# Second feed-forward of a macaron block: batches 0 to 3 through a list of rows sorted by expert

## Chip, cores and metric

One core of one Trainium2 chip. The time is the device time of one execution in microseconds. A run of the kernel before took 1052.49 us (median of three, 1050.71 to 1056.52).

## What is computed

A block of three residual parts over x of shape (8, 512, 128), 8 batches of 512 tokens: half a feed-forward, attention, half a feed-forward again.

```python
x = x + 0.5 * ffn(layernorm(x), ...)
x = x + attn(layernorm(x), ...)
x = x + 0.5 * ffn(layernorm(x), ...)

def ffn(x, gate_w, gate_b, w1, b1, w2, b2, w3, b3):   # 8 experts, 128 x 128 each
    logits = einsum('bsd,de->bse', x, gate_w) + gate_b
    probs = softmax(logits, axis=1)                   # over the tokens of a batch
    vals, idx = top_k(probs, 2)
    h = relu(x @ w1[e] + b1[e]); h = relu(h @ w2[e] + b2[e])
    y = relu(h @ w3[e] + b3[e])                       # for every expert e
    w_tok, ind = the chosen probabilities and the choice, per token and expert
    v = einsum('ebso,bse->eo', y, w_tok)              # one vector per expert
    return einsum('bse,eo->bso', ind, v)
```

The output of an expert for a token counts only through the sum v, weighted with the token's probability for that expert. It is zero for all but the two experts a token chose. The attention has 16 heads of 64 on one key and value head.

## The kernel before

Five engines run programs written by hand; each works in its own order and waits on semaphores. Bias and relu follow each product, and products are made exact enough by splitting both sides into a high and a low part: a layer is three products per 512 tokens (high weights with high data, low weights with high data, high weights with low data).

**Feed-forward.** Its unit is one expert on two batches (a pair), 1024 tokens. Each of the two feed-forwards has 32 units (4 pairs x 8 experts), all dense: every expert sees every token. A unit is 18 products of 128 x 512. TensorE (PE) makes layer 1, VectorE (DVE) makes high and low part of its result (`split1`, L1479 and L1485), PE layer 2, ScalarE (ACT) takes it and rounds it (`relu2`, L1162 and L1166), GpSimd (POOL) makes the low part (`split2`, L686), PE layer 3, and DVE multiplies with the token weights and sums (`reduce3`, L1576). The token weights of a unit are broadcast by a DMA from memory (`load_wb`, L511), into one of eight buffers.

The order of the units is written out by `unit_steps` (L410), which every engine walks: in step u stand layer 1 of unit u+2 with its split, layer 2 of unit u+1, layer 3 of unit u, and then whatever `TAIL` (L382) puts behind step u: the last of the attention (reciprocals, scale, out-projection), the turning of the normalized batches, and the choice of experts for batches 4 to 7. That for batches 0 to 3 is made in the attention.

**PSUM** is a ring of four pairs of banks; the uses are numbered in PE's order, and a use waits until the one four before it is drained.

**Attention.** It runs in 32 quads of four heads (g = 0 to 31, NQ = 32, four per batch). In each, PE makes for eight units the scores of quad g+1 for the row maxima (taken by DVE, L1728) and the scores of quad g (exponentials by ACT, L1356), then the sums of quad g-1 (L1011) and the weighing of the values (L1038). Even quads have projections of q besides, and one in four has k, v and the out-projection (L1050). POOL adds the exponentials (`add_exp`, L627), six sums per quad, which PE's sums need. Exponential u of quad g waits for a sum of quad g-1, because it overwrites what that sum reads.

**SP** issues nearly all DMAs, in one order: in each quad the sums of the last one are spread (`spread_sums`, four transfers, L570), and their reciprocals, taken by DVE, are sent and broadcast (`send_reciprocals`, L576 and L580). After the last quad `late_weights` (L539) mixes the same for quad 31 with the loads of the token weights.

## Time and profile before

| | us |
|---|---|
| median of three runs | 1052.49 |
| lowest, highest | 1050.71, 1056.52 |
| profiled execution, its span (first to last instruction) | 1048.3 |
| TensorE busy | 1015.9 (97%) |
| VectorE, GpSimd, ScalarE busy | 763.9, 700.0, 632.1 |

No time of the profiled execution beyond its span is on the page; what lies around it is taken as the median less the span, 4.2 us. The span falls into the first feed-forward (to some 175 us), the attention (to 877 us, 32 quads of about 16 to 29 us) and the second feed-forward. PE's sum of busy time counts overlapping instructions once; two products in a row start 0.23 us apart although each is listed with 0.39. "SPq" rows are the issuing of DMAs by SP, not their transfer.

### The profile page before, as it was taken

Reading aid. Unit: us, or ns where it says so; the run is one execution under the profiler, and the core shown is the slowest. Engines: PE = TensorE matmul, PEld = TensorE weight load, DVE = VectorE, ACT = ScalarE, POOL = GpSimd, SP = SyncE. Lnnn points to the kernel's source line nnn. Section 1 sums busy time; section 2 is a strip of 40 time slices with the busy share of each in tenths; the row PEclk is TensorE's granted clock in tenths of the full one; section 3 lists DMA queues with packets and bytes.
Section 4 is the critical chain, followed back from the end, with each engine's and each line's share of the span. In section 5 each row is a group of like instructions: output and inputs, shape, how many; then the busy total and the mean of one; then the engine's idle time right before and its main releaser. Section 6 shows DMA issues by size and latency. Waiting matters only on the chain.

```text
span 1048.3 us, 18768 instructions
## 1 busy us (share of the span) xinstructions
PE 1015.9 (97%) x7176; PEld 661.9 (63%) x7176; DVE 763.9 (73%) x1027; ACT 632.1 (60%) x900; POOL 700.0 (67%) x369
## 2 busy tenths in 40 slices
PE   7999998899999999999999999999999999998996
PEld 6676886545657566556655665745565565776884
DVE  6879998877875676567576587546757636779996
ACT  4785556756754565456475477467746456775553
POOL 5555655766886588488488578756849757565653
PEclk9999999999999999999999999999999999999999
DMA  5721520000100100001001010001000103521612
GB/s 169 237 86 58 183 84 21 1 2 23 42 23 22 42 24 22 22 23 43 22 23 43 3 42 23 22 25 40 22 23 23 42 25 102 182 81 49 209 67 81
DMA packets 30253, 59.62 MB, mean 57 GB/s; under 512 B 10437, under 2 KB 15702, under 8 KB 30166
## 3 DMA queue, kind: packets, MB, share of 16 engines
q1 hardware_dynamic: 30096, 58.41, 18.4%
q8 instruction: 58, 0.95, 0.4%
q14 instruction: 29, 0.24, 0.1%
q10 hardware_dynamic: 70, 0.02, 0.0%
HBM read 55.27 MB, written 2.62 MB: 55 GB/s over the span
## 4 chain that ended last, share of the span: by engine, by line
PE 83%; DVE 10%; ACT 2%; issue 2%; POOL 2%; DMA 0%; DVEq 0%; ACTq 0%; POOLq 0%
PE ring L1038 20%; PE ring L972 6%; PE ring L1050 6%; PE ring L996 5%; PE ring L1002 5%; PE ring L998 5%; PE ring L1000 5%; PE ring L742 4%; PE ring L748 4%; PE ring L744 4%; PE ring L1011 3%; PE ring L766 2%; PE ring L765 2%; PE ring L768 2%; DVE ring L1576 2%
## 5 line engine op out<-in xcount | busy, mean ns | idle before, releaser
L1728 DVE TENSOR_REDUCE mx<-ring 128x2 f32<-128x1024 f32 x248 | 290.3, 1226 | 64.1 <-PE ring L972 64.1
L627 POOL TENSOR_TENSOR sum_picksT<-sum_picksT,P_wb 128x1024 f32<-128x1024 f32 x128 | 310.7, 2427 | 18.9 <-POOL sum_picksT L627 0.9
L1356 ACT ACTIVATE P_wb<-ring 128x1024 f32<-128x1024 f32 x256 | 262.1, 1026 | 54.2 <-PE ring L1002 24.6
L627 POOL TENSOR_TENSOR sum_picksT<-P_wb 128x1024 f32<-128x1024 f32 x64 | 167.0, 2610 | 167.8 <-ACT P_wb L1356 167.8
L686 POOL TENSOR_TENSOR R<-t,R 128x512 fp32r<-128x512 f32 x124 | 162.1, 1308 | 124.5 <-ACT R L1166 121.2
L1038 PE MATMUL ring<-P_wb,t 128*32 128x512 f32 x2048 | 228.4, 593 | 0.0
L1038 PEld LDWEIGHTS ring<-P_wb,t 128*32 128x32 f32 x2048 | 74.0, 110 | 138.6 <-issue 120.0
L1368 ACT COPY OZ<-ring 128x512 f32<-128x512 f32 x64 | 37.4, 585 | 157.3 <-PE ring L1038 148.6
L1166 ACT CAST R<-t 128x512 fp32r<-128x512 f32 x124 | 76.9, 620 | 74.6 <-PE ring L748 68.2
L972 PE MATMUL ring<-R 64*128 64x512 f32 x512 | 104.8, 407 | 1.0 <-ACT P_wb L1344 0.7
L996 PE MATMUL ring<-R 64*128 64x512 f32 x512 | 102.0, 393 | 1.5 <-DVE MR L1733 1.5
L1000 PE MATMUL ring<-R 64*128 64x512 f32 x512 | 101.1, 390 | 0.0
L998 PE MATMUL ring<-R 64*128 64x512 f32 x512 | 101.0, 390 | 0.0
L1002 PE MATMUL ring<-MR,NEG 64*128 64x512 f32 x496 | 98.3, 392 | 0.0
L1162 ACT ACTIVATE t<-ring,bcol 128x512 f32<-128x512 f32 x124 | 84.8, 684 | 20.8 <-PE ring L768 20.3
L1576 DVE SCALAR_TENSOR_TENSOR ring<-ring,nb,P_wb 128x1024 f32<-128x1024 f32 x62 | 80.0, 1290 | 13.3 <-PE ring L748 13.2
L742 PE MATMUL ring<-R,whi 128*128 128x512 f32 x252 | 81.5, 404 | 6.1 <-DVE MR L1485 1.8
L748 PE MATMUL ring<-R,whi 128*128 128x512 f32 x252 | 79.6, 396 | 0.0
L744 PE MATMUL ring<-R,wlo 128*128 128x512 f32 x252 | 79.6, 396 | 0.0
L972 PEld LDWEIGHTS ring<-R 64*128 64x128 f32 x512 | 48.2, 184 | 36.9 <-issue 24.9
L1753 DVE TENSOR_TENSOR OT_xnT<-OZ,rzb 128x1024 f32<-128x1024 f32 x32 | 70.0, 2188 | 0.0
L996 PEld LDWEIGHTS ring<-R 64*128 64x128 f32 x512 | 47.9, 184 | 34.6 <-ACT P_wb L1356 29.7
(199 smaller groups left out, 1529.9 us busy)
## 6 DMA issues: line engine op xcount, KB each, us to landing
P_wb<-wd SPq DMA_DIRECT2D x64, 512.0 KB, 4.8
rzb<-rzd SPq DMA_DIRECT2D x64, 256.0 KB, 3.9
xs<-in_L_attn_x SPq DMA_DIRECT2D x8, 256.0 KB, 5.2
zrc<-SZ SPq DMA_DIRECT2D x128, 2.0 KB, 1.7
out<-xs SPq DMA_DIRECT2D x8, 256.0 KB, 2.7
sum_picksT<-in_L_ffn_w SPq DMA_DIRECT2D x2, 512.0 KB, 5.6
MR<-mT SPq DMA_DIRECT2D x62, 4.0 KB
t<-in_L_ffn_w SPq DMA_DIRECT2D x1, 512.0 KB, 7.3
```

The lines of the kernel that those rows point to most:

```text
L627: pool.tensor_tensor(US[:, g % 2, c, :, :], first, PU[:, TPB * c + t, :, :], ALU.add).then_inc(s_ua, 1)
L686: pool.tensor_tensor(low[:, k, :], t2[:, k, :], high[:, k, :].bitcast(F32), ALU.subtract).then_inc(s["h2_ready"], 1)
L742: pe.matmul(pair[:, k, :], whi[:, layer, e, :], high[:, k, :], start=True, stop=False)
L744: pe.matmul(pair[:, k, :], wlo[:, layer, e, :], high[:, k, :], start=False, stop=False)
L972: mm = pe.matmul(banks[:, par, :], QH[g % len(QH)][rows, c, P * j:P * (j + 1)], KH[rows, g // QUADS % 2, :], start=True, stop=True)
L996: pe.matmul(banks[:, par, :], KH[rows, kv, keys], QH[g % len(QH)][rows, c, :], start=True, stop=False)
L998: pe.matmul(banks[:, par, :], KH[rows, kv, keys], QL[g % len(QL)][rows, c, :], start=False, stop=False)
L1000: pe.matmul(banks[:, par, :], KL[rows, kv, keys], QH[g % len(QH)][rows, c, :], start=False, stop=False)
L1002: mm = pe.matmul(banks[:, par, :], less[rows, :], MR[rows, g % 2, c, :], start=False, stop=True)
L1038: mm = pe.matmul(weigh_bank(g, c)[row:row + SLOT, :], Vn[:, g // QUADS % 2, t, d:d + SLOT], PU[:, TPB * c + t, par, :], start=(t == 0), st ...
L1356: act.activation(PU[:, u, :, :], ring[slot(("scores", g, u))][:, :, :], ACT.Exp, scale=SCALE).then_inc(s_exp, 1)
L1728: dve.tensor_reduce(mx[:, :, u] if g else mx0_unit[:, u // TPB, :, 0, u % TPB, 0], ring[slot(("max", g, u))][:, :, :], AX.X, ALU.max).then ...
```

## The change

Batches 0 to 3 of the second feed-forward no longer go through all experts. The two rows each token has (one per chosen expert) are put into a list in memory, sorted by expert, each expert's share padded to full tiles of 512 rows. With 4096 rows and 8 experts that is at most 15 tiles (`RT`), a number fixed when the kernel is built. Two tiles form a unit: 8 sorted units (`RU`), the last with one tile, then the 16 dense ones of batches 4 to 7. The parts:

- In the first feed-forward the list is filled with zeros by five DMAs from SP (`zero_rows`).
- In quad 24 (`CHOICE0`; 28 before) DVE chooses the experts and counts per row what was chosen before it; two small products (`ranks`) give the sums over partitions; in quad 25 `place_rows` works out each row's place in the list, in quad 29 `tile_tables` the expert and the biases of each tile. Turning, logits and probabilities of batches 0 to 3 move two quads ahead.
- ACT writes the normalized rows with their eight token weights beside them into a ring of six (`fill_rows`, quads 25 to 29), and POOL sends them by indirect DMAs of 128 rows of 136 values (`send_rows`): one group of three tiles (six DMAs) behind the sums of quad 25, two groups behind those of 26 and of 28, and the last, of one tile, behind those of 30. POOL then copies the weights of unit 0.
- In the second feed-forward a sorted unit needs: its rows loaded (`load_sorted`, SP), turned (`gather`, eight transposes on PE), split (`sorted_high` on ACT, `sorted_low` on DVE), its token weights picked out by DVE, written and broadcast (`spread_row_weights`, SP), and the weights of its two tiles' experts copied by POOL to a fixed place (`copy_weights`), since they are known only at run time. The token-weight buffers are a ring of three there. Split and reduction go in halves, because the two tiles have different biases.
- `TAIL` has the rest of the attention and the choice for batches 4 to 7 behind steps 0 to 7.

The core of the diff:

```diff
+    TS = 4 * P
+    RT = 2 * TPB * TPB * P // TS + E - 1
+    RU = (RT + 1) // 2
+    UNITS_OF = (NU, RU + NU // 2)
...
+        PLACES0, TILES0 = NQ - 7, NQ - 3
+        ROWS_FILLED = {NQ - 7: (0, 1), NQ - 6: (2,), NQ - 5: (3,), NQ - 4: (4,), NQ - 3: (5,)}
+        ROWS_SENT = {NQ - 7: (0,), NQ - 6: (1, 2), NQ - 4: (3, 4), NQ - 2: (5,)}
...
+        TAIL = {0: [("copy", 3), ("scale", NQ - 1), ("normal", 4)],
+                1: [("copy", 4), ("out", B - 1), ("turn", 4), ("normal", 5)],
...
+                7: [("choose", 1), ("choose", 2), ("choose", 3), ("picks", 1)]}
...
-                steps = [("layer1", 0), ("split", 0), ("sums", NQ - 1), ("normal", 2), ("layer1", 1), ("split", 1), ("layer2", 0)]
+                steps = [("copy", 1), ("layer1", 0), ("split", 0), ("sums", NQ - 1), ("gather", 1), ("layer1", 1), ("split", 1),
+                         ("reciprocals", NQ - 1), ("gather", 2), ("layer2", 0), ("copy", 2)]
...
+                if routed(f, u + 3):
+                    steps.append(("gather", u + 3))
...
+            def spread_row_weights(u):
+                n = len(halves_of(1, u))
+                sp.wait_ge(s_rw, u + 1)
+                sp.dma_start(wg[u, 0:n].rearrange("k p j -> p k j"), row_weights[u % 2][:, 0:n, :]).then_inc(s_rwd, 16)
+                sp.wait_ge(s_rwd, 16 * (u + 1))
...
             def late_weights():
+                s = F[1]
                 spread_sums(NQ - 1)
+                load_sorted(1)
+                spread_row_weights(0)
                 send_reciprocals(NQ - 1)
+                for u in range(2, RU):
+                    load_sorted(u)
+                    spread_row_weights(u - 1)
+                spread_row_weights(RU - 1)
+                send_weights(1, 1, GW[1][1]["wT"])
...
+            def send_rows(n):
+                pool.wait_ge(s_fill, n + 1)
...
+                for i, t in enumerate(FILLS[n]):
+                    for k in range(2):
+                        place = TPB * TPB * k + t
+                        pool.indirect_dma_start(out=xg[:, :], out_offset=bass.IndirectOffsetOnAxis(ap=row_of[:, place:place + 1], axis=0),
+                                                in_=ring_rows[:, FILL * (n % 2) + i, :], in_offset=None).then_inc(s_sent[n % 2], 16)
+            def copy_weights(u):
...
+                for k in halves_of(1, u):
+                    e = pool.value_load(expert_int[0:1, 2 * u + k:2 * u + k + 1], min_val=0, max_val=E - 1)
+                    ins = pool.tensor_copy(tile_weights(u, k).rearrange("p l h o -> p (l h o)"),
+                                           wex[:, bass.ds(e, 1), :, :, :].rearrange("p e l h o -> p (e l h o)"))
+                ins.then_inc(s_tw, 1)
...
             def layer1(f, u):
+                if routed(f, u):
+                    pe.wait_ge(s_rxl, u + 1)
+                    pe.wait_ge(s_tw, u + 1)
...
+            def gather(u, pair):
+                pe.wait_ge(s_sorted[u % 2], 16 * (u // 2 + 1))
+                for half in halves_of(1, u):
+                    mm = turn(pair[:, half, :], lambda j: sorted_of(u)[:, half, j, 0:P])
+                mm.then_inc(s_rx, 1)
```

TensorE at the start of the second feed-forward; `P_wb,t` is the weighing of quad 31, `sum_picksT,ones` are its sums, `ident` rows are transposes, and a layer is three or six rows. Before:

```order
L1038 MATMUL ring<-P_wb,t 32x512 x32
L742 MATMUL ring<-R,whi 128x512 x2
L744 MATMUL ring<-R,wlo 128x512 x2
L748 MATMUL ring<-R,whi 128x512 x2
L1011 MATMUL ring<-sum_picksT,ones 32x512 x4
L742 MATMUL ring<-R,whi 128x512 x2
L744 MATMUL ring<-R,wlo 128x512 x2
L748 MATMUL ring<-R,whi 128x512 x2
L765 MATMUL ring<-R,whi 128x512
L766 MATMUL ring<-R,wlo 128x512
L768 MATMUL ring<-R,whi 128x512
```

And now:

```order
L1234 MATMUL ring<-sum_picksT,ones 32x512 x4
L1075 MATMUL ring<-ident,sum_picksT 128x128 x8
L959 MATMUL ring<-R,tile_weights 128x512 x2
L961 MATMUL ring<-R,tile_weights 128x512 x2
L965 MATMUL ring<-R,tile_weights 128x512 x2
L1075 MATMUL ring<-ident,sum_picksT 128x128 x8
L986 MATMUL ring<-R,first_tile_weights 128x512
L987 MATMUL ring<-R,first_tile_weights 128x512
L989 MATMUL ring<-R,first_tile_weights 128x512
```

Between the sums and layer 2 of unit 0 (L765 before, L986 now) there was one layer; now there are two gathers and a layer between them.

SP after the last quad's reciprocals; `rows_by_expert` is the sorted list, `weights_by_row` the picked token weights. Before:

```order
L570 DMA zrc<-SZ 16x1x32 x4
L511 DMA P_wb<-wd 128x1024 x2
L576 DMA rzd<-zrc 64x32
L580 DMA rzb<-rzd 64x1024 x2
L511 DMA P_wb<-wd 128x1024 x12
```

And now:

```order
L737 DMA zrc<-SZ 16x1x32 [waits reciprocals,sums_taken]
L737 DMA zrc<-SZ 16x1x32 x3
L679 DMA sum_picksT<-rows_by_expert 128x2x544 [waits sums_filled]
L685 DMA weights_by_row<-tile_tables 128x2x4 [waits row_weights_ready]
L692 DMA P_wb<-weights_by_row 128x1024 [waits exp_added,pv_done,row_weights_written]
L743 DMA rzd<-zrc 64x32 [waits reciprocals]
L747 DMA rzb<-rzd 64x1024 [waits quad_scaled,reciprocals_written]
L747 DMA rzb<-rzd 64x1024
L679 DMA sum_picksT<-rows_by_expert 128x2x544 [waits row_weights_ready,sorted_turned,sums_filled]
```

The load for gather 1 stands behind the spreading of quad 31's sums, that for gather 2 behind its reciprocals.

POOL from the sums of quad 31 on; `tile_weights` are the copied weights, `h_low` and R the low parts ahead of layer 3. Before:

```order
L627 TENSOR_TENSOR sum_picksT<-P_wb 128x1024
L627 TENSOR_TENSOR sum_picksT<-sum_picksT,P_wb 128x1024 x2
L686 TENSOR_TENSOR R<-t,R 128x512 x4
L660 TENSOR_TENSOR R<-sum_picksT,R 128x512
L686 TENSOR_TENSOR R<-t,R 128x512 x2
```

And now:

```order
L794 TENSOR_TENSOR sum_picksT<-P_wb 128x1024
L794 TENSOR_TENSOR sum_picksT<-sum_picksT,P_wb 128x1024 x2
L889 TENSOR_LOAD tile_tables
L889 ISA x2
L890 ISA
L890 COPY tile_weights<-wex 128x768
L889 TENSOR_LOAD tile_tables
L889 ISA x2
L890 ISA
L890 COPY tile_weights<-wex 128x768
L856 TENSOR_TENSOR h_low<-t,R 128x512 x2
L889 TENSOR_LOAD tile_tables
```

A copy for two tiles now stands between the low parts of one unit and those of the next.

## Rows read from the trace of the kernel before

**Rows 1.** Page of the profile, busy time of each engine and share of the span

```profile
PE 1015.9 (97%) x7176; PEld 661.9 (63%) x7176; DVE 763.9 (73%) x1027; ACT 632.1 (60%) x900; POOL 700.0 (67%) x369
```

**Rows 2.** Windows: second feed-forward to unit 15; columns PE, PEld, DVE, ACT, POOL busy, clock, DMA

```profile
877.00:973.00 96.00, 91.36 (x427) 69.57 (x427) 78.58 (x101) 64.17 (x117) 53.86 (x40) 1.00 0.38 123
```

**Rows 3.** Timeline (start, duration us, engine, line): one dense unit, 975.4 to 979.6

```profile
975.41 0.63 PE L742 MATMUL ring<-R,whi 128*128 128x512 f32 x2
...
975.68 1.29 DVE L1576 SCALAR_TENSOR_TENSOR ring<-ring,nb,P_wb 128x1024 f32<-128x1024 f32 x1 [0.24 <-PE ring L748]
...
976.30 2.59 POOL L686 TENSOR_TENSOR R<-t,R 128x512 fp32r<-128x512 f32 x2 [1.59 <-ACT R L1166]
...
979.61 0.63 PE L742 MATMUL ring<-R,whi 128*128 128x512 f32 x2
```

**Rows 4.** Timeline, DVE: the end of the last unit

```profile
1037.17 0.20 DVE L1688 TENSOR_REDUCE vv<-vacc 128x8 f32<-128x40 f32 x1
```

**Rows 5.** Timeline, PE: out-projection of quad 30, eight transposes, sums of quad 31

```profile
844.89 7.41 PE L1050 MATMUL ring<-wos,OT_xnT 128*128 128x128 f32 x64
...
867.84 1.09 PE L854 MATMUL ring<-ident,xn 128*128 128x128 f32 x8
...
879.44 1.06 PE L1011 MATMUL ring<-sum_picksT,ones 128*32 128x512 f32 x8 [1.04 <-POOL sum_picksT L627]
```

**Rows 6.** Timeline, ACT and the DMA issues of SP behind those sums

```profile
880.56 0.59 ACT L1362 COPY SZ<-ring 128x512 f32<-128x512 f32 x1 [3.11 <-PE ring L1011]
...
881.17 2.44 SPq L570 DMA_DIRECT2D zrc<-SZ  x4
```

**Rows 7.** DMA issues, 860 to 1048: count, KB each, median us from issue to landing

```profile
P_wb<-wd SPq DMA_DIRECT2D x32, 512.0 KB, 5.0
...
rzd<-zrc SPq DMA_DIRECT2D x2, 8.0 KB, 1.7
```

**Rows 8.** Timeline, DVE: split of two 128x1024 as four 128x512, and a scale

```profile
807.62 2.84 DVE L1722 SCALAR_TENSOR_TENSOR R<-ring,bcol,R 128x512 fp32r<-128x512 f32 x4 [1.34 <-ACT R L1337]
...
888.99 1.79 DVE L1753 TENSOR_TENSOR OT_xnT<-OZ,rzb 128x1024 f32<-128x1024 f32 x1
```

**Rows 9.** Timeline, POOL: operations with one input or none

```profile
0.27 0.11 POOL L1878 MEMSET const-float32-1.0<- 128x1 f32 x1
...
1.19 0.29 POOL L614 TENSOR_SCALAR_AFFINE_SELECT ident<-ident 128x128 f32<-128x128 f32 x1 [0.24 <-POOL ident L612]
```

**Rows 10.** Windows, 25 to 35; columns as in rows 2

```profile
25.00:30.00 5.00, 3.64 (x10) 2.49 (x10) 4.93 (x7) 2.24 (x5) 0.77 (x2) 0.74 0.42 156
30.00:35.00 5.00, 5.00 (x21) 4.01 (x21) 4.96 (x14) 2.05 (x4) 2.04 (x3) 0.91 1.01 288
```

**Rows 11.** Timeline, POOL: first sum of quads 26 to 31, with the idle time before it

```profile
753.17 2.40 POOL L627 TENSOR_TENSOR sum_picksT<-P_wb 128x1024 f32<-128x1024 f32 x1 [2.23 <-ACT P_wb L1356]
...
782.54 2.40 POOL L627 TENSOR_TENSOR sum_picksT<-P_wb 128x1024 f32<-128x1024 f32 x1 [14.53 <-ACT P_wb L1356]
...
800.09 2.40 POOL L627 TENSOR_TENSOR sum_picksT<-P_wb 128x1024 f32<-128x1024 f32 x1 [1.42 <-ACT P_wb L1356]
...
821.01 2.40 POOL L627 TENSOR_TENSOR sum_picksT<-P_wb 128x1024 f32<-128x1024 f32 x1 [3.81 <-ACT P_wb L1356]
...
839.12 2.40 POOL L627 TENSOR_TENSOR sum_picksT<-P_wb 128x1024 f32<-128x1024 f32 x1 [2.28 <-ACT P_wb L1356]
...
863.47 2.40 POOL L627 TENSOR_TENSOR sum_picksT<-P_wb 128x1024 f32<-128x1024 f32 x1 [9.58 <-ACT P_wb L1356]
```

**Rows 12.** Timeline, ACT: the exponentials of quad 30

```profile
836.86 9.17 ACT L1356 ACTIVATE P_wb<-ring 128x1024 f32<-128x1024 f32 x8 [0.75 <-POOL sum_picksT L627]
```

**Rows 13.** Timeline, DVE: choice of experts in quad 28, first and last, next row maxima

```profile
810.58 0.27 DVE L1616 TENSOR_REDUCE tm<-ring 128x16 f32<-128x128 f32 x1
...
814.50 0.37 DVE L1610 TENSOR_TENSOR wtk<-ind,ring 128x128 f32<-128x128 f32 x1
...
817.83 9.34 DVE L1728 TENSOR_REDUCE mx<-ring 128x2 f32<-128x1024 f32 x8 [1.51 <-PE ring L972]
```

More of the change, by code:

```diff
@@ new lines, in macaron_kernel @@
+        before = tables[:, 0:P]
+        ring_rows = tables[:, P:P + 2 * FILL * ROW].rearrange("p (t c) -> p t c", c=ROW)
+        up_to = [tables[:, P + 192 * k:P + 192 * (k + 1)] for k in range(2)]
+        products = tables[:, 4 * P:6 * P].rearrange("p (k t e) -> p k t e", k=2, e=E)
+        row_of_all = tables[:, 6 * P:7 * P].rearrange("p (t e) -> p t e", e=E)
+        LEFT = P + 2 * FILL * ROW
+        count_up = tables[:, LEFT:LEFT + 2 * E]
+        running = [tables[:, LEFT + 2 * E + 12 * k:LEFT + 2 * E + 12 * (k + 1)] for k in range(4)]
@@ new lines, in macaron_kernel @@
+        first_choice, second_choice = (lg0[:, P * k:P * (k + 1)].rearrange("p (t e) -> p t e", e=E) for k in range(2))
+        chosen_by_p, counts, before_p, tiles_full, first_row = (lg0[:, 2 * P + E * k:2 * P + E * (k + 1)] for k in range(5))
+        counts_and_before = lg0[:, 2 * P + E:2 * P + 3 * E]
+        full = lg0[:, 2 * P + 5 * E:2 * P + 9 * E].rearrange("p (e k) -> p e k", k=4)
+        row_sums = lg0[:, 2 * P + 9 * E:2 * P + 13 * E].rearrange("p (k t) -> p k t", k=2)
+        row_of = lg0[:, S - 4 * E:S].bitcast(I32)
@@ L692, in units @@
                         split2(f, arg)
+                    elif stage == "copy":
+                        copy_weights(arg)
                     elif stage == "turn":
@@ L871, in early_gate @@
                     else:
-                        turn_weights(1, 0, bank[:, 0:P])
+                        pe.wait_ge(s_places, 1)
+                        pe.wait_ge(s_const, 5)
+                        pe.matmul(bank[:, 0:E], ones[:, :], chosen_by_p, start=True, stop=True)
+                        pe.matmul(bank[:, E:2 * E], before, chosen_by_p, start=True, stop=True).then_inc(s["picks_transposed"], 1)
             def first_turns():
-                s = F[1]
                 wait_drained(pe, "first_turns")
-                for b in range(2):
-                    pe.wait_ge(s["xn_done"], b + 1)
-                    turn(ring[slot("first_turns")][:, b, :], lambda k: xn[:, b, k, :]).then_inc(s["xn_transposed"], 1)
+                gather(0, ring[slot("first_turns")])
             def units(f):
@@ L894, in units @@
                             sums(arg, bank)
+                        elif stage == "gather":
+                            gather(arg, unit_pair(f, stage, arg))
                         elif stage == "turn":
@@ L1115, in attention @@
                         elif step == "first_turns":
[L1116 removed]
+                            pass
                         elif step == "out":
@@ L1405, in attention @@
                     early_gate(g, 0)
-                    if g == NQ - 1:
-                        for b2 in range(2):
-                            act.wait_ge(F[1]["xn_transposed"], b2 + 1)
-                            act.copy(xh[:, b2, :], ring[slot("first_turns")][:, b2, :]).then_inc(F[1]["x_high"], 1)
                     if g:
```

655 lines of the change are left out of this document (444 added, 211 removed).

## The prediction, made blind

> **What bounds the kernel now.** I read the page first: TensorE is busy 97% of the span [rows 1]. Then the windows: over the half of the second feed-forward that the change rewrites, TensorE is busy 91.4 of 96.0 us and VectorE 78.6, at full clock [rows 2]. The timeline of one dense unit shows the pace: its 18 products take from 975.41 to 979.61, 4.2 us, 1.4 a layer. VectorE needs three passes of 1.29 (the reduction is one), so it has almost nothing to spare [rows 3]. Beside it stands the order of the changed kernel, which I went through wait by wait: on a path that crosses engines what counts is who stands behind whom. The last unit ends at 1037.17 [rows 4].
>
> **What goes.** 16 dense units become 8 sorted ones, of which one is half: 8.5 units x 4.2 = 35.7 us of products. This is the whole gain. I count it from S, the start of the sums of quad 31 (879.44 before [rows 5]), to the end of the reduction of the seventeenth dense unit before (975.68 + 1.29 [rows 3] + the accumulator's 0.1 = 977.1, so S + 97.6) and of unit 8, the first dense one, after. From there both have 15 dense units and the same end (977.1 to 1037.17).
>
> **Head of the second feed-forward.** TensorE's order is now: layer 1 of unit 0, sums, gather 1, layer 1 of unit 1, gather 2, and only then layer 2 of unit 0. From S: ScalarE has the sums at 881.15, SP issues four small transfers until 883.61 [rows 6], S + 4.2. Only behind them comes the load of sorted rows 1; it has 0.56 MB, and I give it the 5.0 of the 0.5 MB transfers [rows 7]: 9.2. Gather (eight transposes) 1.1 [rows 5], ScalarE's high part over 1024 columns 1.1 (the exponentials' pace, 9.17 for 8 [rows 12]), VectorE's low part 1.3 [rows 3]: 12.7. Layer 1 1.4, its split, now four passes, 2.8 [rows 8]: 16.9. Now VectorE scales quad 30, 1.8 [rows 8], and inverts the sums of quad 31 (small, left out): 18.7. SP stands waiting for that inverse: write 1.7 [rows 7], two issues of 0.6 [rows 6], and behind them the load of sorted rows 2, 5.0: 26.6. Gather 1.1: layer 2 of unit 0 starts at S + 27.7. All of it is one path; nothing runs beside it but the split of unit 0 and a weight copy.
>
> **The steps.** POOL's order is: low parts of unit u+1, copy of the weights of unit u+3, and layer 1 of unit u+3 waits for that copy, with layer 2 of unit u+2 behind it. The high part of unit u+1 is written only after layer 3 of unit u. In the dense unit POOL's two low parts end at 976.30 + 2.59 = 978.9, 3.5 after layer 3 was issued (975.41) [rows 3]; the 1.59 that POOL idles ahead of them is that wait. So each step is a ring: 3.5, copies K, three layers 4.2. For K no row has the operation: two copies of 768 columns and two values read from a table. A POOL pass with one input takes 0.29 for 128 columns, an almost empty one 0.11 [rows 9]: 0.11 + 768 x 0.18/127 = 1.2 each. The read lies between nothing and 1.7 (a small transfer [rows 7]); I take 0.35, near nothing, since it moves four bytes. K = 3.1, bounds 2.0 (copies at 1.0, reads free) and 7.1 (copies as two-input passes of 1.84, between 1.3 a 512 pass [rows 3] and 2.40 a 1024 one [rows 11], reads at 1.7).
> TensorE then idles some 5 us in each ring. In the first feed-forward, where it is busy 3.64 of 5 us, the clock falls: 0.74 and then 0.91 of full over ten us [rows 10]. At half clock 0.26 x 5 x 2 + 0.09 x 5 x 2 = 3.5 us, in which half is lost: 1.7. I charge 1.7 per ring; bounds 0 and 4.2 (all three layers at half clock, 1.2 GHz).
> The Trainium skill (TensorE: Matmul & The Clock Gate, "Why this matters for your kernels") warns of exactly this: idle gaps between bursts of products send the array back to half rate. The rows of the first feed-forward bear it out; by the opposite reading, clock never lost, the sum is 10 us lower.
> The first ring from 27.7: ScalarE still has the high part of gather 2 (1.1), four passes of 0.6 [rows 6], 2.5; POOL's second low part 1.3; K 3.1; 4.2 + 1.7: layer 3 of unit 0 is issued at 41.6. Ring = 3.5 + 3.1 + 4.2 + 1.7 = 12.5: 54.1. The second ring holds the out-projection, 7.3 [rows 5], a turn 0.4, a gather 1.1 and the three layers, 4.2, 13.1 in all at full clock: 67.2. Two more: 92.2. In the fifth K is halved (unit 7 has one tile): 10.9, 103.1. Unit 6 needs no copy: 4.2, 107.3. VectorE alone would need, per sorted unit, 1.3 + 0.6 for the sorted rows, 2.8 for the split and 1.7 for two reductions, 6.4: it is covered, as are ScalarE and the gathers.
>
> **From the sorted to the dense units.** The choice for batches 4 to 7 is now squeezed into steps 5 to 7. Reduction of unit 6 1.7, inverse and probabilities 0.9, their turn 0.4, first links 1.2, split of unit 9 2.6, half reduction 0.9: 115.0. Ten links of 0.33 (14 passes from 810.58 to 814.87 [rows 13]), turn and copy 0.6, 118.9; write of the weights 1.7 (as the small write of rows 7), broadcast 5.0, reduction 1.4: 127.0. Before, this chain ran beside units that had their weights; now the first dense reduction waits for it. 127.0 - 97.6 = +29.4.
>
> **In the attention.** VectorE gets 22 memsets (0.1 each, my value from POOL's 0.11 [rows 9]) and six links of 0.33 in quad 24, 4.2 us, beside the choice moved there. In quad 28 it idled 1.51 behind the same choice [rows 13]: +2.7, bounds 0 and 4.2; in this phase row maxima run at TensorE's pace and regain nothing.
> POOL sends 32 times 128 rows: 6 behind quad 25, 12 behind 26, 12 behind 28, 2 behind 30, then copies K. No row has such a send. Bounds are SP's issue, 0.6 [rows 6], and a small transfer whole, 1.7 [rows 7]; I take the middle, 1.1. Against the gaps [rows 11] POOL is late by 6.6 - 2.2 = 4.4, + 13.2 - 14.5 = 3.1, - 1.4 = 1.7, + 13.2 - 3.8 = 11.1, - 2.3 = 8.8, + 2.2 + 3.1 - 9.6 = 4.5. The exponentials of quad 30 (836.86 [rows 12]) need only the first sum of quad 29, 823.4 [rows 11], so 11.1 is inside the 13.4 allowed; the 4.5 reaches the sums of quad 31, which waited for POOL before too (1.04 [rows 5]): +4.5. At 0.6 it is 0; at 1.7 POOL is 29.1 late, quad 30 stands 15.7, and 8.0 is left at the end: 23.7.
> The Trainium skill (DMA: Bandwidth & Descriptors, "Latency and other measured facts") gives about 1 us until the first byte of a software-made transfer, and lays it on descriptor making. No row here shows it; at 1.0 the term would be 1.4 and the time 3 us less.
> The zeroing transfers lie beside dense units whose weights are loaded eight units ahead, ScalarE's 16 row passes between its waits for the weighing: nothing.
>
> **Sum.** 29.4 + 2.7 + 4.5 = +36.6 on the span of 1048.3: 1084.9. The runs' median lies 4.2 above that span: 1089 us.
>
> **Rivals.** (a) Sends cost 1.7: the last term is 23.7 instead of 4.5, 1108. For it: POOL makes them itself, 12 in a gap of 3.8. Against: only two of the five gaps are short. (b) Weight copies are cheap and the clock holds: K = 2.0 in 5.5 rings saves 6, no clock loss 10, sends free 4.5, 1068. For it: the table is tiny, and nothing shows that a read or a send holds POOL at all. (c) The other side: the ring doesn't close, because copies run ahead of POOL's low parts and the loads land before they are asked for. Then VectorE paces, 6.4 x 7.5 = 48 plus 12 for its other work, 10 at the head and 12 for the weights of the first dense unit: S + 82, 15.6 less than before; with 7 for the attention -8.4, 1044. It decides from a ring below about 7.5; against it stands the order itself, 3.5 + 4.2 + any copy. (d) The change doesn't do what it says: the number of tiles, 15, is fixed when the kernel is built, so I give this nothing.
>
> **How the numbers follow.** Forecast 0.55, its own range 1073 to 1107 (K from 2.0 to 5, sends up to 1.3). (a) 0.17, (b) 0.14, (c) 0.08, and 0.06 for a mixture that ends near the time before, split evenly between no change and a small loss. The runs spread by 0.5%, so within 5 us of 1052.5 is what can't be told from no change. Faster 0.08, same 0.03, slower 0.89. From 1060 to 1116 lie all of the forecast, most of (a) and (b); some 2 in 10 are outside.
>
> **What would show it.** Right: TensorE idle for 5 us or more ahead of gathers 1 and 2, released by a load; ahead of layer 1 of units 2 to 7, released by POOL's copy; row of the first dense reduction released by a transfer; clock below 1 in the sorted stage; layer 3 to layer 3 in 11 to 14 us. Wrong: layer 3 to layer 3 in 6 to 8 us with VectorE without gaps, layer 2 of unit 0 before S + 15, or exponentials of quads 28 to 30 that wait long for POOL.

## The result, and the profile after

The changed kernel takes 1097.06 us (median of four runs, 1096.3 to 1101.05), the one before 1052.3 us in the same session: a ratio of 1.0433, 95% interval 1.0405 to 1.0461. The forecast was 1089 us, range 1060 to 1116. The profiled execution has a span of 1094.3 us against 1048.3.

The first part of the page of the changed kernel, busy time by engine, against [rows 1]:

```profile
PE 1004.6 (92%) x7070; PEld 650.3 (59%) x7070; DVE 765.2 (70%) x1100; ACT 615.4 (56%) x873; POOL 716.4 (65%) x400
```

TensorE is busy 11 us less, 92% of the span instead of 97%. Where it stands still is in the windows of the second feed-forward (start and end, length, busy time and number of instructions of each engine, TensorE's granted clock, share of the DMA engines, GB/s):

```profile
core 0: us, PE busy (x) PEld busy (x) DVE busy (x) ACT busy (x) POOL busy (x), PEclk, DMA share, GB/s
897.00:940.00 43.00, 17.09 (x58) 12.21 (x57) 13.58 (x21) 6.82 (x9) 5.63 (x6) 0.56 0.38 102
940.00:997.00 57.00, 42.92 (x220) 32.31 (x219) 37.27 (x69) 31.21 (x57) 28.28 (x25) 0.97 0.20 66
997.00:1022.00 25.00, 14.77 (x50) 11.45 (x49) 17.71 (x33) 7.25 (x14) 3.81 (x3) 0.73 0.14 43
1022.00:1094.00 72.00, 64.29 (x283) 49.26 (x281) 60.87 (x71) 38.17 (x61) 38.71 (x30) 0.97 0.40 133
```

Three stages stand between the sums of quad 31 and the steady dense units: the head (26 of 43 us idle, clock 0.56 of full), the sorted units, and the choice for batches 4 to 7. Before, this part had hardly a gap [rows 2].

For accounting I cut the kernel at two instants that both kernels have: the sums of quad 19 and S, the sums of quad 31. From the one to the other it takes 246.9 us before (632.57 to 879.44) and 262.7 after (634.18 to 896.89); from S to the end of the span 168.9 and 197.4. The remaining 1.6 us lie ahead of the sums of quad 19; they belong to no part of the change, since kernels with the same code up to there have this instant anywhere from 632.4 to 639.5.

**The head.** TensorE in the changed kernel, from S to the first layer 2 (start, duration, engine and line, tile written and read, shape, count, and in brackets the idle time ahead and what ended it):

```profile
896.89 1.06 PE L1234 MATMUL ring<-sum_picksT,ones 128*32 128x512 f32 x8 [1.54 <-POOL sum_picksT L794]
905.62 1.94 PE L1075 MATMUL ring<-ident,sum_picksT 128*128 128x128 f32 x8 [7.66 <-DMA sum_picksT<-rows_by_expert]
925.47 1.94 PE L1075 MATMUL ring<-ident,sum_picksT 128*128 128x128 f32 x8 [12.63 <-DMA sum_picksT<-rows_by_expert]
927.06 0.78 PE L986 MATMUL ring<-R,first_tile_weights 128*128 128x512 f32 x1
```

and SyncE, which issues the transfers one behind the other:

```profile
898.62 2.43 SPq L737 DMA_DIRECT2D zrc<-SZ  x4
901.10 0.59 SPq L679 DMA_DIRECT2D sum_picksT<-rows_by_expert  x1
901.73 0.46 SPq L685 DMA_DIRECT2D weights_by_row<-tile_tables  x1
905.70 0.33 SPq L692 DMA_DIRECT2D P_wb<-weights_by_row  x1
917.15 0.49 SPq L743 DMA_DIRECT2D rzd<-zrc  x1
918.85 1.12 SPq L747 DMA_DIRECT2D rzb<-rzd  x2
920.08 0.52 SPq L679 DMA_DIRECT2D sum_picksT<-rows_by_expert  x1
```

Both gathers wait for a load, and both loads stand in SyncE's queue: rows 1 behind the four transfers of the sums, rows 2 behind a wait for the reciprocals of quad 31 (917.15). Nothing that the loads need was missing: in a run below both are issued by S + 4.3.

**The sorted units.** Around layer 1 of unit 3, GpSimd's low parts and copy, VectorE's scale and then the product that waited:

```profile
942.03 2.56 POOL L856 TENSOR_TENSOR h_low<-t,R 128x512 fp32r<-128x512 f32 x2 [7.85 <-ACT R L1381]
943.53 2.14 DVE L2092 TENSOR_TENSOR OT_xnT<-OZ,rzb 128x1024 f32<-128x1024 f32 x1
944.54 2.58 POOL L890 CAST tile_weights<-wex 128x768 fp32r x2
947.22 1.19 PE L959 MATMUL ring<-R,tile_weights 128*128 128x512 f32 x2 [5.05 <-issue]
```

The ring of the prediction is there: low parts, copy, and only then layer 1. The "issue" of 5.05 us is the wait for the copy, which ended at 947.12. Two copies take 2.58 here and 1.59 or 1.60 for six other units.

**The choice.** The last two large waits, and the first dense reduction:

```profile
1002.57 1.09 PE L1075 MATMUL ring<-ident,OZ 128*128 128x128 f32 x4 [4.30 <-ACT OZ L1409]
1015.21 0.45 PE L1039 MATMUL ring<-ident,wtk 128*128 128x128 f32 x1 [5.93 <-DVE wtk L1976]
1022.00 1.29 DVE L1835 SCALAR_TENSOR_TENSOR ring<-ring,nb,P_wb 128x1024 f32<-128x1024 f32 x1 [0.26 <-PE ring L965]
```

**The attention.** Quad 25: VectorE works out the rows' places; beside it GpSimd, ScalarE and TensorE:

```profile
747.25 2.32 DVE L1903 TENSOR_TENSOR lg<-lg,tables 128x32 f32<-128x32 f32 x1
749.60 0.19 DVE L1905 TENSOR_REDUCE tables<-lg 128x8 f32<-128x32 f32 x1
749.82 2.25 DVE L1908 TENSOR_TENSOR tables<-tables 128x8 f32<-128x8 f32 x1
752.10 0.17 DVE L1908 TENSOR_TENSOR tables<-tables 128x8 f32<-128x8 f32 x1
752.30 2.29 DVE L1908 TENSOR_TENSOR tables<-tables 128x8 f32<-128x8 f32 x1
754.63 1.21 DVE L1909 SCALAR_TENSOR_TENSOR lg<-tables,lg 128x8 f32<-128x8 f32 x1
```

```profile
747.14 2.37 POOL L794 TENSOR_TENSOR sum_picksT<-P_wb 128x1024 f32<-128x1024 f32 x1
749.66 4.90 POOL L794 TENSOR_TENSOR sum_picksT<-sum_picksT,P_wb 128x1024 f32<-128x1024 f32 x2
754.53 1.28 POOL L800 TENSOR_TENSOR R<-xn,R 128x512 fp32r<-128x512 f32 x1
758.58 0.58 ACT L1595 COPY OZ<-ring 128x512 f32<-128x512 f32 x1 [10.53 <-DVE OT_xnT L2092]
762.26 0.79 PE L1219 MATMUL ring<-R 64*128 64x512 f32 x2 [6.52 <-ACT OZ L1595]
```

Operations on 8 to 32 columns take 1.2 to 2.3 us, and each ends when GpSimd's operation beside it ends: L1903 at 749.57 (GpSimd 749.51), L1909 at 755.84 (755.81). Of the three adds the first takes 2.25 and ends at 752.07 (752.05), the third 2.29 and ends at 754.60 (754.57). The second, which fell into the 0.14 us between two of GpSimd's sums, takes 0.17, and an addition of 128x128 right behind GpSimd's last operation (L1912) takes 0.29. The same operation on the same kind of inputs is slow or quick by what GpSimd does. The reduction's 0.19 says nothing by itself, since it began in such a gap too. The whole chain takes 10.8 us (746.53 to 757.36), ScalarE stands 10.53 behind it and TensorE 6.52.

Behind quad 28: the end of twelve sends, the first sum of quad 29 behind them, and the exponentials that wait for it:

```profile
844.58 0.96 POOL L875 DMA_INDIRECT rows_by_expert<-tables,lg  x1 [0.30 <-issue]
845.84 1.05 POOL L875 DMA_INDIRECT rows_by_expert<-tables,lg  x1 [0.30 <-issue]
846.92 2.40 POOL L794 TENSOR_TENSOR sum_picksT<-P_wb 128x1024 f32<-128x1024 f32 x1
849.43 1.94 ACT L1583 ACTIVATE P_wb<-ring 128x1024 f32<-128x1024 f32 x2 [1.24 <-POOL sum_picksT L794]
```

A send holds GpSimd for 0.96 us, and one starts 1.26 behind another. From 768.2 us to S GpSimd has no idle time.

### The profile page after: what moved, and what is told of

Read it like the earlier page. It is cut to its first block, busy times and chain, and to the rows that moved or that the text cites. A ratio compares the mean times of both kernels' runs of the same rounds, so it can differ in the third digit from the quotient of the medians.

```text
span 1094.3 us, 18664 instructions
## 1 busy us (share of the span) xinstructions
PE 1004.6 (92%) x7070; PEld 650.3 (59%) x7070; DVE 765.2 (70%) x1100; ACT 615.4 (56%) x873; POOL 716.4 (65%) x400
## 3 DMA queue, kind: packets, MB, share of 16 engines
q0 software_dynamic: 1024, 2.23, 0.7%
## 4 chain that ended last, share of the span: by engine, by line
PE 66%; POOL 12%; DVE 10%; issue 5%; ACT 4%; DMA 2%; SPq 0%; POOLq 0%; DVEq 0%; ACTq 0%
PE ring L1261 15%; POOL sum_picksT L794 9%; PE ring L1195 5%; PE ring L1219 4%; PE ring L1225 4%; PE ring L1221 4%; PE ring L1223 4%; PE ring L1273 4%; PE ring L959 4%; PE ring L961 4%; PE ring L965 4%; POOL rows_by_expert L875 3%; PE ring L1234 2%; PE ring L986 2%; PE ring L987 2%
## 5 line engine op out<-in xcount | busy, mean ns | idle before, releaser
L794 POOL TENSOR_TENSOR sum_picksT<-sum_picksT,P_wb 128x1024 f32<-128x1024 f32 x128 | 312.2, 2439 | 18.7 <-POOL sum_picksT L794 0.4
L794 POOL TENSOR_TENSOR sum_picksT<-P_wb 128x1024 f32<-128x1024 f32 x64 | 164.0, 2562 | 138.4 <-ACT P_wb L1583 138.3
L856 POOL TENSOR_TENSOR h_low<-t,R 128x512 fp32r<-128x512 f32 x105 | 135.4, 1290 | 166.0 <-ACT R L1381 165.7
L1381 ACT CAST R<-t 128x512 fp32r<-128x512 f32 x111 | 68.8, 620 | 66.8 <-PE ring L965 61.2
L1376 ACT ACTIVATE t<-ring,bcol 128x512 f32<-128x512 f32 x96 | 65.7, 684 | 23.0 <-PE ring L989 22.5
L2092 DVE TENSOR_TENSOR OT_xnT<-OZ,rzb 128x1024 f32<-128x1024 f32 x32 | 67.1, 2098 | 5.6 <-DMA rzb<-rzd 5.6
L1835 DVE SCALAR_TENSOR_TENSOR ring<-ring,nb,P_wb 128x1024 f32<-128x1024 f32 x46 | 59.4, 1291 | 11.1 <-PE ring L965 11.1
L959 PE MATMUL ring<-R,wex 128*128 128x512 f32 x188 | 62.3, 413 | 4.1 <-DVE R L1721 1.6
L961 PE MATMUL ring<-R,wex 128*128 128x512 f32 x188 | 60.4, 403 | 0.0
L2079 DVE CAST mT<-ring 16x128 fp32r<-16x128 f32 x31 | 8.6, 276 | 72.6 <-PE ring L1240 50.4
```

The costliest lines, as they stand in the source:

```text
L794: pool.tensor_tensor(US[:, g % 2, c, :, :], first, PU[:, TPB * c + t, :, :], ALU.add).then_inc(s_ua, 1)
L856: pool.tensor_tensor(low[:, k, :], t2[:, k, :], high[:, k, :].bitcast(F32), ALU.subtract).then_inc(s[f"h2_low{k}"], 1)
L959: pe.matmul(pair[:, k, :], weights_of(f, u, k, layer, 0), high[:, k, :], start=True, stop=False)
L961: pe.matmul(pair[:, k, :], weights_of(f, u, k, layer, 1), high[:, k, :], start=False, stop=False)
```

## The experiments

Times of each against the kernel before on the same chip (its medians there: 1051.47 to 1052.05 us); "634 to S" and "S to end" are the two stretches above, from the profiled execution. That execution need not be the median one: it lies 6.9 us above the median for "places in PSUM" (whose five runs go from 1090.61 to 1102.3) and 3.5 above for "rows 1, 2 early", so stretches and medians don't add up to a tenth. The times of "places in PSUM" and "no sends" can't be told from that of the changed kernel (their intervals overlap its own); what they show is read from the stretches.

| kernel | us | ratio, 95% interval | 634 to S | S to end |
|---|---|---|---|---|
| before | 1052.3 | 1 | 246.9 | 168.9 |
| changed | 1097.06 | 1.0433 (1.0405 to 1.0461) | 262.7 | 197.4 |
| places in PSUM | 1095.43 | 1.0407 (1.0375 to 1.0439) | 260.9 | 199.9 |
| no sends | 1094.37 | 1.0400 (1.0366 to 1.0433) | 259.8 | 199.6 |
| both | 1086.42 | 1.0324 (1.0297 to 1.0350) | 252.9 | 198.9 |
| sums on TensorE | 1101.77 | 1.0479 (1.0437 to 1.0520) | 265.6 | 198.2 |
| copies first | 1087.63 | 1.0341 (1.0311 to 1.0371) | 262.7 | 189.1 |
| rows 1, 2 early | 1083.71 | 1.0300 (1.0270 to 1.0329) | 262.9 | 189.5 |
| rows three ahead | 1076.13 | 1.0245 (1.0219 to 1.0271) | as changed | 175.5 |
| warm TensorE | 1091.20 | 1.0378 (1.0358 to 1.0397) | 262.9 | 192.7 |
| four together | 1069.36 | 1.0164 (1.0147 to 1.0181) | 260.0 | 175.4 |
| all together | 1074.44 | 1.0210 (1.0174 to 1.0246) | 266.1 | 172.1 |
| best | 1062.75 | 1.0103 (1.0086 to 1.0120) | 259.9 | 167.1 |
| best, no sends | 1056.77 | 1.0043 (1.0027 to 1.0060) | 252.9 | 166.3 |

### Attention: places in PSUM, no sends, both

The edits, here and below, are shortened.

```diff
+                use(("turn", PLACES0), ..., (s_places, 3))
-  tensor_tensor(running[k + 1], running[k], running[k] shifted)      # all in SBUF
+  tensor_copy(running[k], scan[k])
+  tensor_tensor(scan[k + 1], scan[k], running[k] shifted)            # scan: PSUM
...
-  pool.indirect_dma_start(out=xg[:, :], ...)                         # 32 of them
+  pool.memset(ring_rows[:, FILL * (n % 2), 0:1], 0.0)                # one a group
```

> The changed kernel; the chain that works out the rows' places in quad 25 keeps its short intermediates in PSUM (in the free half of a bank of that quad), so that none of its two-input operations up to the adding of the row of an expert reads both inputs from SBUF; four more copies. Theory 'held operation': two-input operations of VectorE on SBUF stand until GpSimd's running sum has ended; the chain of 10.8 us falls to about 5, ScalarE takes the weighing of quad 25 some 6 us earlier, the interval between the sums of quads 24 and 25 (37.8 us) falls to 31 or 32, S from 896.9 to about 891, the time by 6 (1091). Rival 'length of the chain': it is its number of links and their place in the order that cost; the chain stays at 10 or more, nothing is gained.

> The changed kernel without its 32 sends of rows (a one-column memset stands for each group, so the sorted list stays as it was filled; everything else as it is). Theory 'GpSimd paces the end of the attention': it has no idle time from 768 to 897 us, and 26 sends of 1.26 us stand in it; without them quad 30 loses its 5.0 us and quad 31 its 1.6, S falls by 7 to 9, the time to about 1089. The wait for the places in quad 25 (6.5 us of TensorE) stays. Rival 'sends are hidden': S moves by less than 2. The prediction's own term for the sends was 4.5.

> The two experiments of the attention together: the places' intermediates in PSUM, and no sends of rows. Alone the first gave 7.3 us in quad 25 but lost 4 again where GpSimd was waited for, the second 2.9. Theory 'each hides the other': GpSimd's sends are what the earlier places ran into, so together they give more than the sum of what each gave from the sums of quad 19 (634) to S: that stretch, 262.7 in the changed kernel, 260.9 and 259.8 with each alone, falls to 248 to 251 (before: 246.9), the time to about 1085. Rival 'independent': 258, the time about 1093.

In the first of these the same links, now one input of each in PSUM, beside the same kind of sum on GpSimd, and ScalarE behind them:

```profile
754.20 0.17 DVE L1916 TENSOR_TENSOR ring<-ring,tables 128x8 f32<-128x8 f32 x1
755.42 0.17 DVE L1918 SCALAR_TENSOR_TENSOR ring<-tables,ring 128x8 f32<-128x8 f32 x1
756.93 1.54 DVE L1926 CAST lg<-lg 128x32 int32<-128x32 f32 x1
753.51 2.39 POOL L795 TENSOR_TENSOR sum_picksT<-P_wb 128x1024 f32<-128x1024 f32 x1
759.69 0.58 ACT L1596 COPY OZ<-ring 128x512 f32<-128x512 f32 x1 [4.87 <-DVE OT_xnT L2101]
```

An add of 128x8 takes 0.17 us while GpSimd's sum runs (753.51 to 755.90), where two of three took 2.3; the chain has five copies more and takes 5.2 us (753.30 to 758.47), of which 1.5 is a last copy within SBUF that was held in turn (0.18 in the changed kernel, where GpSimd stood idle). The interval from the sums of quad 24 to those of quad 25 falls from 37.8 to 30.5, as expected. That is the "held operation". The time gives back most of it: the interval from the sums of quad 28 to those of 29, in which the exponentials of quad 30 stand, grows from 29.8 to 32.0 and the last one from 12.2 to 14.1, because GpSimd, full of sends, is reached earlier. Another 1.4 us stand in the interval from the sums of quad 23 to those of 24. Of the kernels with this edit only this one and "sums on TensorE" have them, five others don't, so they aren't counted as its price; their cause is open. Without the sends alone the gain is 2.9 us; with both it is 9.8, more than 1.8 (2.8 in "four together" and "best", up to S) and 2.9 together. The rival "independent" is out: two causes in a row, each hidden behind the other. What both leave, 6.0 us, is not a single wait: 3.1 lie between the sums of quads 19 and 24, ahead of places and sends, where the work that the change moved two quads forward now stands, and 2.2 are won back in later quads; 1.5 are left in the interval of the places, 2.8 in that from the sums of 28 to those of 29, where TensorE waits 2.25 for a row maximum, and 0.8 in the last. No run tests these.

### Sums on TensorE: a miss

```diff
+        LEFT_TO_PE = {26: 2, 28: 2, 29: 1, 30: 2}
-                for t in range(1, TPB):                 # add_exp, GpSimd
+                for t in range(1, TPB - left):
+    parts = [US[...]] + [PU[:, UNITS - 1 - k, par, :] for k in range(left)]   # sums, PE
```

> The changed kernel with the places' intermediates in PSUM, all sends kept, and seven of GpSimd's running sums given to TensorE (the last one or two exponentials of quads 26, 28, 29 and 30 are added in the sums' products on TensorE, where two more products each cost about 0.3 us). Theory 'GpSimd paces from quad 26 on': 7 x 2.4 = 17 us of its work go while TensorE gets 2; the stretch from 634 to S falls from 260.9 to 252 or 253, as without any send (252.9), the time to about 1086. Rival 'the sends themselves (their DMAs, their queue) slow the quads': no more than 2 us.

It is 4.7 us above the changed kernel, and 6.3 above "places in PSUM", whose edit it has too. The sums of quad 28 on TensorE in this kernel, and ScalarE's exponentials that now wait for them:

```profile
838.64 1.05 PE L1240 MATMUL ring<-sum_picksT,ones 128*32 128x512 f32 x4
840.38 1.92 PE L1240 MATMUL ring<-P_wb,ones 128*32 128x512 f32 x6
842.42 1.94 ACT L1591 ACTIVATE P_wb<-ring 128x1024 f32<-128x1024 f32 x2 [4.97 <-PE ring L1240]
843.50 3.64 PE L1267 MATMUL ring<-P_wb,t 128*32 128x512 f32 x32 [1.20 <-ACT P_wb L1591]
```

The 16 records of products (10 are in these lines) take 3.7 us instead of 1.06 for 8: accumulating ones for the same rows start 0.43 us apart, not beside each other. With the wait of 1.2 it should be 3.8 us a quad. That full price shows only between the sums of quads 26 and 27 (24.7 us instead of 20.7 with the places alone); in the three last intervals it is -0.6, +0.9 and +0.4, where the relief of GpSimd paid for most of it. GpSimd did get idle time (12.8 us ahead of its sums of quad 31), so work was taken off it, but the engine that took it over had less to spare.

### Second feed-forward: copies first, rows early, rows three ahead, warm TensorE

```diff
-    steps = [("copy", 1), ("layer1", 0), ...                 # copies first
+    steps = [("copy", 1), ("copy", 2), ("copy", 3), ("layer1", 0), ...
+                if u and routed(f, u + 3):
+                    steps.append(("copy", u + 3))
                 steps.append(("layer2", u + 1))
...
+                load_sorted(1)                               # rows 1, 2 early
                 spread_sums(NQ - 1)
-                load_sorted(1)
+                load_sorted(2)
                 spread_row_weights(0)
...
+                for u in range(RU):                          # rows three ahead, besides the two above
+                    write_row_weights(u)
+                    if u + 3 < RU: load_sorted(u + 3)
+                    if u == 1: send_reciprocals(NQ - 1); load_row_weights(0)
+                    if u: load_row_weights(u)
...
+                if u in {1: 48, 2: 80, 3: 14}:               # warm TensorE
+                    warm(pair[:, 0, :], WARM[u])
...                                                    # and 30, 26, 36 at three other waits
```

> The changed kernel; GpSimd copies the weights of unit u+3 ahead of the low parts of unit u+1 instead of behind them (the first three copies at the head). Theory 'ring through the copy': layers 1 and 2 no longer wait for high part, low part and copy in a row; from layer 3 of unit 0 to that of unit 6 the stage takes about 45 us instead of 57.2, the clock stays higher, the time falls by 8 to 12. Rival 'only the copy itself': 1.6 us a ring, at most 7 in all. Rival 'the choice of batches 4 to 7 is next': TensorE's waits for it grow by what is saved, the time falls by 0 to 3.

> The changed kernel; SyncE asks for the sorted rows of unit 1 ahead of the spreading of the sums of quad 31, and for those of unit 2 right behind it. Theory 'head by the order of the transfers': gather 1 no longer waits (7.66 us), gather 2 waits for a few us instead of 12.6; layer 2 of unit 0 starts at about S + 15 instead of S + 30.2; the time falls by 12 to 15. Rival 'given back later': the ring and the choice for batches 4 to 7 take it back, less than 5.

> The changed kernel; SyncE asks for the sorted rows three units ahead and no longer stands behind the write of the token weights: rows of unit 1 ahead of the sums of quad 31, rows 2, write of weights 0, rows 3, write 1, rows 4, and only then the reciprocals. With rows 1 and 2 alone moved, gather 3 stood 15.0 us for its rows (S + 26). Theory 'the head is SyncE's queue': gather 3 stands no more than 3 us, layer 3 of unit 0 starts near S + 26 instead of S + 42.7 (with rows 1 and 2 alone S + 30), the time falls below 1080. Rival 'reciprocals and choice pace': they come later by the transfers put ahead of them; what the head gains is lost ahead of the out-projection and the time stays at 1084.

> The changed kernel with transposes of the unit matrix in TensorE's waits (48, 80 and 14 ahead of gathers 1, 2 and 3, 30 ahead of layer 1 of unit 3, 26 and 36 ahead of the turns of the probabilities and of the picks). Theory 'clock': the granted clock from S to the first dense reduction rises from 0.6 to 0.8 to nearly 1, and the products behind the waits that run at half rate (about 5.3 instead of 2.8 us for two layers) come back to full: 6 to 9 us less. That is the term of 1.7 us a ring of the prediction. Rival 'the waits absorb it': the products behind a wait are faster, but the next wait is longer by as much, below 3 us.

Copies first gave 9.4 us. From the layer 3 of unit 0 to that of unit 6 it takes 51.4 us instead of 57.2 (the first step 5.1 instead of 11.9, the next then 14.5 with its out-projection); I expected 45. The ring is open, and the steps behind it do not get shorter: 9.4 and 12.3 us between layers 3 in the middle, with waits of 2.1 at each product of logits.

Rows 1 and 2 early gave 13.4 us by the medians (7.9 from S to the end in its profiled execution, the slowest of four), but gather 3 now stood 15.0 us for its rows, whose load was issued at 915.45, behind the same reciprocals. With rows three units ahead no gather waits: layer 3 of unit 0 starts at S + 22.0 instead of S + 42.7, and the time falls by 20.9 us, 22 from S to the end. TensorE's waits for probabilities and picks are 4.3 and 5.9 us in these three and in the changed kernel, to a tenth: they hang on the steps of the list, not on when the list starts.

The warm kernel lets TensorE turn a unit matrix while it waits. Its windows over the head, against 0.53 (897 to 927) and 0.68 (927 to 942) of the changed kernel:

```profile
895.00:925.00 30.00, 21.91 (x163) 19.36 (x164) 7.93 (x14) 2.43 (x3) 1.77 (x3) 0.89 0.28 77
925.00:940.00 15.00, 11.69 (x71) 10.09 (x70) 8.43 (x13) 6.98 (x13) 6.08 (x6) 0.89 0.46 140
```

The granted clock rises to 0.89, and the time falls by 5.9 us, 4.7 of it from S to the end. So the clock was a loss of its own, of about 5 us.

### Together

"Four together" has places, copies, rows three ahead and the choice a unit earlier; "all together" adds the sums on TensorE, a new order of the choice and reciprocals sent ahead of rows 4; "best" leaves those sums out and adds warm transposes.

> Four changes at once: places' intermediates in PSUM, weight copies ahead of the low parts, SyncE's order with rows three units ahead, and the out-projection, the turning and the choice for batches 4 to 7 each about one unit earlier (picks behind unit 6 instead of 7). Theory: the losses are separate terms of one path, so it is 1097 - 3 (places) - 9 (copies) - 17 (loads) - up to 8 (choice) = 1060 to 1065. Rival 'one bound behind all': the weights of the first dense unit need the choice, whose chain of some 35 us starts with the reciprocals of quad 31; then the time stays above 1072.

> All together: places in PSUM, seven running sums on TensorE, weight copies ahead of the low parts, rows three units ahead on SyncE with the reciprocals ahead of rows 4, batches 4 to 6 turned ahead of and around the out-projection, logits of batch 7 in step 3 and the choice in steps 4 to 6. Against 1069.4 with four of these: 7 to 8 us from the running sums, 5 from the out-projection that no longer waits for the first reduction (7.2 us), up to 8 from the waits for probabilities and picks (3.6 and 5.1). Theory: 1050 to 1055, no slower than the kernel before by more than what a measurement can tell. Rival 'VectorE paces the sorted units': the waits of the choice move into the units, 1060 to 1064.

> The last combination without the running sums on TensorE (they cost it 6 us ahead of S), and with transposes of the unit matrix in three waits (30 ahead of the out-projection, 20 and 18 ahead of the turns of probabilities and picks). From S to the end 172.1 us were left with the new order of the choice (175.4 without), and the stretch from 634 to S should be back at 260. Expected: 1068 from these two, less 1 to 3 for the clock, 1065 to 1067, the best of the sorted kernels and still above the one before. If the order of the choice had gained nothing by itself, it stays at 1069.

> The same without the 32 sends of rows (the list stays as it was filled): what the sorted kernel would be worth if sending cost nothing. The stretch from 634 to S falls to 253, the time to 1058 to 1060. Theory 'two separate losses': it is still above the 1052 of the kernel before, by what the second feed-forward loses in TensorE's waits (S to the end 172 against 168.9) and the places in the attention. Rival 'the sends were all of it': 1052 or less.

```diff
+  TAIL = {0: [("turn", 4), ("normal", 5), ("scale", NQ - 1), ("out", B - 1), ("turn", 5), ("logits", 4), ...],   # best
+          1: [("moments", 8), ("root", 8), ("turn", 6), ("logits", 5)],
+          2: [("invert", 8), ("logits", 6), ("normal", 7)],
+          3: [("turn", 7), ("logits", 7), ("largest", 1), ("exp", 1)],
+          4: [("invert_sum", 1), ("probs", 1), ("turn_probs", 1), ("choose", 0)],
+          5: [("choose", 1), ("choose", 2), ("choose", 3)],
+          6: [("picks", 1)],
+          8: [("routed", 1)]}
```

Four together came to 1069.36, above the 1060 to 1065 expected: S to the end was 175.4, no less than with rows three ahead alone. A new wait stood there, 7.2 us ahead of the out-projection, whose scale VectorE did only behind the first reduction, and that waited for token weights queued behind the reciprocals. With the reciprocals ahead and the choice spread as above it is 172.1, but the sums on TensorE cost more than that gave, 1074.44. Without them and with warm transposes ahead of the out-projection and the choice it is 1062.75, the best of the sorted kernels, better than expected (1065 to 1067): behind S the transposes are its only difference from all together, and they give 5.0 us there, not 1 to 3. Its dense part starts in time: the windows of the stage that had 0.73 of the clock and 10 us of waits:

```profile
930.00:970.00 40.00, 32.11 (x143) 22.76 (x143) 28.83 (x56) 23.37 (x39) 17.92 (x17) 0.91 0.25 81
970.00:985.00 15.00, 12.32 (x61) 9.19 (x60) 14.28 (x25) 6.00 (x11) 4.90 (x4) 1.00 0.13 40
```

The last pair was expected to show two separate losses, the feed-forward among them. It shows one: with 167.1 and 166.3 us the second feed-forward is now 2 us faster than before (168.9), and what keeps the kernel behind is the attention, 13.0 us, 7 of which the sends make. No version beats the one before.

## Why the prediction was right, and where not

**The path from S to the first dense unit: right, +29.4 forecast, +28.5 measured.** Step by step, from S, with the issue of layer 3 taken as its start and 1.4:

| | forecast | measured |
|---|---|---|
| layer 2 of unit 0 | 27.7 | 30.2 |
| layer 3 issued, units 0 to 6 | 41.6, 54.1, 67.2, 79.7, 92.2, 103.1, 107.3 | 44.1, 56.0, 68.6, 78.1, 88.8, 96.6, 101.2 |
| first dense reduction ended | 127.0 | 126.4 |

The end agrees better than its terms, and that is luck: the head is 2.5 too short and the choice 5.5, the steps between them are 8.6 too long. The head was 2.5 late: the load of rows 1 took 4.5 where 5.0 was assumed, but the two gathers ran at half rate, 1.94 instead of the 1.1 of [rows 5], and the reciprocals went out at S + 20.3, not 18.7.

**The ring: right in kind, its copy mis-sized.** K was taken as 3.1 with 2.0 as the lower bound; it is 1.6, so the true value lay outside the bounds. I scaled a copy from an operation of 128 columns [rows 9]; two of 768 columns take 0.80 each with the reading of the table in it. With 1.6 and a full clock the ring would be 9.3, and no step shows it bare: the first two took 11.9 and 12.6, and with copies first, in the open order, they are 4.9 us shorter together; the third takes 9.5 in the changed kernel and 9.4 there, so it was the logits that set it. The copies-first run shows that the ring did bind at the start (9.4 us in all), and that opening it does not bring VectorE's 6.4 us a unit: 7.4 at best, in the best kernel.

**The clock: 1.7 us a ring forecast, at another place in fact.** Over units 1 to 6 the clock is 0.97; it is lost in the head and in the choice (0.56 and 0.73). The warm kernel puts it at some 5 us in all (5.9 by the medians, 4.7 behind S), the forecast at about 10. The Trainium skill (TensorE: Matmul & The Clock Gate, "Why this matters for your kernels") says that idle gaps send the array back to half rate; the trace agrees behind the gaps of 4.3 to 12.6 us (the products after each start 0.43 apart, against 0.23 at full clock), and in units 2 to 6, with waits of 1 to 2 us, the clock stayed full.

**The choice: 5.5 us too short, hidden by steps that were too long.** From the last sorted layers to the first dense reduction I had 19.7 us (107.3 to 127.0), it took 25.2 (101.2 to 126.4). I expected the transfer of the weights to be last; the reduction waited for TensorE (0.26), which itself had stood 5.9 for the picks.

**The attention: wrong, +7.2 forecast, +17.4 measured.** Of the 17.4, 1.6 lie ahead of the sums of quad 19, as said. Two terms of the forecast failed. VectorE's share counted the 22 memsets and six links in quad 24, which cost nothing there (20.68 us against 20.58 between the sums of quads 23 and 24; four of the links, with both inputs in SBUF, took 0.29 each, GpSimd being idle), and the twelve operations that work out the places in quad 25 were left out altogether: at 0.33 each they would be 4.0 us, they took 10.8, and the PSUM run takes 7.3 us back in that interval. The Trainium skill (SBUF — State Buffer, "Who interferes with whom") says that a VectorE instruction with two SBUF inputs contends with a GpSimd instruction that reads SBUF, and calls the port pair they share an exclusive lock; the adds of quad 25 (2.25 and 2.29 us beside GpSimd's sums, 0.17 between them) and the PSUM run bear it out. It speaks against this change and was not weighed. That is the step that failed, here and in the whole prediction: a chain without a term, and a price per link that was read from rows with one input in PSUM [rows 13] and holds within SBUF only beside an idle GpSimd.

The second term is the sends. I took 1.1 us, at 1.7 it would have been rival (a); it is 1.26, and at that size the exponentials of quad 30 do wait for GpSimd: the forecast's reserve of 13.4 us was used up by the 12 sends behind quad 28 (15.9 us, 831.01 to 846.89), with lateness brought from earlier quads. The wait is short, 3.3 us in three pieces. Without sends 2.9 us come back alone, 7.0 to 8.0 with the places out of the way. The median lies 2.8 us above the profiled span, where 4.2 was added.

**The signs.** TensorE did stand 7.66 and 12.63 us ahead of gathers 1 and 2, released by a load, and the clock was below 1. Ahead of layer 1 it stood 5.05 us for a copy at unit 3 alone, and 1.4 or less for one at the other units; layer 3 to layer 3 took 11 to 14 us in two of six steps (11.9, 12.6, then 9.5, 10.6, 7.9, 4.6); and the first dense reduction was released by TensorE, not by a transfer. So the ring bound in fewer steps than the forecast had it. Of the signs of being wrong one came, the exponentials of quad 30 waiting for GpSimd, and it points at the attention.

**The rivals.** (a), sends at 1.7, is refuted by the size of a send; that the time lies nearly halfway to it comes mostly from the places. (b), all cheap, had the copy nearest and was right on the clock of the sorted units; it was wrong on the head, the choice and the sends. (c) needed the ring not to close; the copies-first run makes it so and stays at 1087, since the head and the choice are there as well. It took four more changes to bring the stage near VectorE's pace, and even then the whole kernel won nothing by it.

## What to carry to other kernels

When work is taken out of a stage that ran without a gap, first follow each queue that the replacement has to pass in order: here a load of rows stood behind a wait of 11 us that had nothing to do with it. Moving the first two loads ahead was worth 13 of the 45 us lost, asking for all rows three units ahead 21. Count every small link of a chain, ask what the engine beside it does meanwhile, and put one input in PSUM where GpSimd is busy. And look for pairs of losses in a row: taking one away alone shows 2 or 3 us, both together 10.

## What the runs showed of the hardware that I had not expected

- An operation of VectorE with two SBUF inputs, or a copy from SBUF to SBUF, waits until GpSimd's operation beside it ends: 1.2 to 2.3 us for 8 to 32 columns, 0.17 with an input in PSUM or in the gap between two of GpSimd's sums. A reduction from SBUF to SBUF isn't held: L1925 of the PSUM run takes 0.42 beside GpSimd's sum, as it does in the changed kernel with GpSimd idle. It holds in the other direction too: VectorE's scale over 1024 columns was held by GpSimd's low part (2.14 instead of 1.22, ended 945.67) and held the first of the two weight copies in turn (1.82, the second 0.82).
- An indirect DMA of 128 rows of 544 bytes holds GpSimd for 0.96 us, and they follow each other in 1.26.
- Products with 32 output columns for the same group of rows start 0.43 us apart when they accumulate; eight to four groups take 1.06.
